# Per-head weight products in 16-bit passes: splitting raw weights on ScalarE and VectorE, with one raw buffer in place of two

## The reference

```
q_c = rmsnorm(hidden @ w_qa, g_qa)                # 384 latent columns
q   = q_c @ w_qb           -> q_nope (128), q_rope (64) for each of 32 heads
k_c = rmsnorm(kv[..., :128], g_kva)               # 128 latent columns
kst = k_c @ w_kvb          -> k_nope (128), v (128) for each head
scores = (query . key) * 192**-0.5                # nope and rope parts together
attn   = softmax(scores)
out    = (attn @ v) as 4096 columns @ w_o         # w_o: 4096 x 1024
```

## Time and profile before

| | |
|---|---|
| median of three timed runs | 2040.95 us |
| the profiled execution, its own time | 2044.69 us |
| its span | 2042.9 us |
| PE busy | 1892.5 us, 93% of the span |
| DVE busy | 1321.2 us, 65% |
| ACT busy | 773.2 us, 38% |
| POOL busy | 308.4 us, 15% |

### The profile page before, as it was taken

The page is one execution under the profiler, slowest core; times in us unless marked ns, Lnnn a source line. Parts: engine busy times, 40 slices in busy tenths (PEclk is TensorE's granted clock), DMA queues, the critical chain, the costliest instruction groups (busy, mean ns, idle before and its releaser), DMA issues. The chain is left out here.

```text
span 2042.9 us, 32412 instructions
## 1 busy us (share of the span) xinstructions
PE 1892.5 (93%) x11538; PEld 1029.6 (50%) x11538; DVE 1321.2 (65%) x2742; ACT 773.2 (38%) x2020; POOL 308.4 (15%) x596
## 2 busy tenths in 40 slices
PE   4898898559999999999999999999999999859999
PEld 2344444335555555555555555555555555425554
DVE  4678777436666666666666666666666666555554
ACT  3454554233333334433333433333343333332221
POOL 2376675300000000000000000000000000033332
PEclk9899999679999999999999999999999999979999
DMA  5244342332222322232222222223222222243332
GB/s 143 52 86 96 81 95 65 76 91 51 58 58 59 76 56 53 58 76 59 58 58 55 73 58 58 58 58 75 55 55 58 40 39 39 39 138 80 80 82 73
DMA packets 305609, 138.87 MB, mean 68 GB/s; under 512 B 295088, under 2 KB 295344, under 8 KB 303408
## 3 DMA queue, kind: packets, MB, share of 16 engines
q1 hardware_dynamic: 301136, 108.35, 24.8%
q10 hardware_dynamic: 4320, 28.51, 4.0%
HBM read 56.07 MB, written 8.39 MB: 32 GB/s over the span
## 5 line engine op out<-in xcount | busy, mean ns | idle before, releaser
L1031 PE MATMUL out_ps<-m_h,ot_h 128*128 128x512 f16 x1024 | 389.4, 380 | 1.7 <-DVE ot_l L835 1.7
L1032 PE MATMUL out_ps<-m_l,ot_h 128*128 128x512 f16 x1024 | 389.0, 380 | 0.0
L1033 PE MATMUL out_ps<-m_h,ot_l 128*128 128x512 f16 x1024 | 388.9, 380 | 0.0
L756 ACT ACTIVATE qp_h<-qp_ps 128x512 f16<-128x512 f32 x126 | 75.3, 597 | 492.6 <-PE qp_ps L966 492.6
L812 ACT ACTIVATE prob<-s_ps,nmx 128x128 f32<-128x128 f32 x512 | 181.3, 366 | 207.3 <-DVE nmx L905 207.3
L885 DVE SCALAR_TENSOR_TENSOR resid<-out_ps,resid 128x512 f32<-128x512 f32 x256 | 176.1, 688 | 97.1 <-PE out_ps L1033 97.1
L835 DVE SCALAR_TENSOR_TENSOR qp_l<-qp_ps,qp_h 128x512 f16<-128x512 f32 x126 | 87.2, 692 | 234.5 <-ACT qp_h L756 234.5
L1221 POOL MEMSET fpower<- 128x1 f32 x1 | 0.1, 99 | 1392.4 <-POOLq L674 1392.4
L966 PE MATMUL qp_ps<-lat,wp_h 128*128 128x512 f16 x756 | 205.6, 381 | 0.0
L1033 PEld LDWEIGHTS out_ps<-m_h,ot_l 128*128 128x128 f16 x1024 | 100.4, 98 | 121.6 <-issue 1.4
L1031 PEld LDWEIGHTS out_ps<-m_h,ot_h 128*128 128x128 f16 x1024 | 100.5, 98 | 110.5 <-DVE ot_l L835 2.7
(11 more groups left out here) (217 smaller groups left out, 3861.3 us busy)
## 6 DMA issues: line engine op xcount, KB each, us to landing
wide<-heads_in ACTq DMA_DIRECT2D x30, 928.0 KB, 4.7
wide<-x_in SPq DMA_DIRECT2D x30, 512.0 KB, 6.5
tower_out<-result SPq DMA_DIRECT2D x16, 512.0 KB, 2.6
stage<-wb_in SPq DMA_DIRECT2D x8, 512.0 KB, 8.3
resid<-wqk_in SPq DMA_DIRECT2D x1, 2304.0 KB, 11.6
zt<-z SPq DMA_TRANSPOSE x128, 2.4
turned<-halves SPq DMA_TRANSPOSE x128, 3.0
wide<-heads_in SPq DMA_DIRECT2D x2, 928.0 KB, 4.6
```

The lines of the kernel that those rows point to most:

```text
L756: act.activation(out, src, ACT.Copy, scale=scale).then_inc(done, 1)
L1031: pe.matmul(out_ps[hf][:, :], ot_h[:, h, :], m_h[:, at], start=h == 0, stop=False)
L1032: pe.matmul(out_ps[hf][:, :], ot_h[:, h, :], m_l[:, at], start=False, stop=False)
L1033: last = pe.matmul(out_ps[hf][:, :], ot_l[:, h, :], m_h[:, at], start=False, stop=h == HEADS - 1)
```

## The change

The raw weights of the heads whose products are made inside the rounds are split into 16-bit halves, and the product is made from them in three passes. For that the second raw buffer, wide1, is given up once the first four heads are done: its memory holds both halves of the 1664 columns w_q to w_o. The split is made in three pieces: 640 columns (w_q, w_k, w_v) in slot 0, and 512 each (the halves of w_o) in slots 1 and 2, so each piece is made one slot ahead of the part that reads it. On ScalarE a piece stands behind the split of the probabilities and ahead of the query's, on VectorE behind the additions of outputs and ahead of the query's split. The scale of the split, RAW_S = 2**8 on both operands, is taken out where the product is read. The load of the next head, now always into wide0, moves from the start of slot 0 to the start of slot 3, where the raw row has been split. The diff, cut to its core:

```
+        raw_hi, raw_lo = sem("raw_hi"), sem("raw_lo")
+        split = keep["wide1"][:, :].bitcast(F16)
+        split_h, split_l = split[:, 0:RAW_R], split[:, RAW_R:2 * RAW_R]
+        PIECES = [slice(RAW_Q, RAW_O), slice(RAW_O, RAW_O + CHUNK), slice(RAW_O + CHUNK, RAW_R)]
...
+            def raw_high(h, n):
+                if n == 0:
+                    act.wait_ge(raw_loaded[0], (h - HEADS) * 16 + 48)
+                    act.wait_ge(prod_done, h * 3)
+                    if h == HEADS:
+                        act.wait_ge(wr_lo, HEADS)
+                high(split_h[:, PIECES[n]], keep["wide0"][:, PIECES[n]], RAW_S, raw_hi)
...
             def body(before, now, after, more):
-                if more and (not now.known or now.t + HEADS + 1 < NH):
-                    act.wait_ge(prod_done, now.t * 3 + 3 * HEADS)
-                    act.wait_ge(wr_lo, now.t + HEADS)
-                    load(now.t + HEADS + 1, 1 - now.parity)
                 for j in range(QUAD):
                     s = now.slot + j
+                    if j == QUAD - 1 and now.t + HEADS + 1 < NH:
+                        act.wait_ge(wr_lo, now.t + HEADS + 1)
+                        act.wait_ge(raw_lo, now.t * 3 + 3)
+                        load(now.t + HEADS + 1, 0)
...
                     high(p_h, prob[:, :, :].rearrange("p h n -> p (h n)"), PR_S, p_hi)
+                    if more and j < len(PIECES):
+                        raw_high(now.t + HEADS, j)
                     if after:
                         query_high(after, j)
...
                         add_out(*behind, 1)
+                    if more and j < len(PIECES):
+                        dve.wait_ge(raw_hi, now.t * 3 + (j + 1))
+                        low(split_l[:, PIECES[j]], keep["wide0"][:, PIECES[j]], RAW_S, split_h[:, PIECES[j]], raw_lo)
                     if after:
                         query_low(after, j)
...
+            def split_products(h, part, bank, free):
+                pe.wait_ge(raw_lo, (h - HEADS) * 3 + (part + 1))
+                pe.wait_ge(prod_lo, free)
+                ways = ((split_h, split_h), (split_h, split_l), (split_l, split_h))
+                if part == 0:
+                    for k in range(QT):
+                        for n, (a, b) in enumerate(ways):
+                            last = pe.matmul(bank[:, k * P:(k + 1) * P], a[:, RAW_Q + k * P:RAW_Q + (k + 1) * P],
+                                             b[:, RAW_K:RAW_K + P], start=n == 0, stop=n == 2)
+                else:
+                    at = RAW_O + (part - 1) * CHUNK
+                    for n, (a, b) in enumerate(ways):
+                        last = pe.matmul(bank[:, :], a[:, RAW_V:RAW_V + P], b[:, at:at + CHUNK],
+                                         start=n == 0, stop=n == 2)
+                last.then_inc(prod_done, 1)
...
                     if more and j:
-                        products(now.t + HEADS, now.parity, j - 1, prod_ps, (now.t + HEADS) * 3 + (j - 1))
+                        split_products(now.t + HEADS, j - 1, prod_ps, (now.t + HEADS) * 3 + (j - 1))
```

More of the change, by code:

```diff
@@ L53 @@
 KR_S, QRO_S = 2.0**7, 2.0**7
+RAW_S = 2.0**8
 WP_S, WR_S, M_S = 2.0**9, 2.0**8, 2.0**10
@@ L758, in prod_high @@
             def prod_high(h, p, sd, k, part, bank, fresh):
+                un = 1.0 if fresh else RAW_S ** -2
                 act.wait_ge(prod_done, h * 3 + part + 1)
@@ L762, in prod_high @@
                     high(wp_h[:, bass.ds(sd, 1), :, bass.ds(k, 1), :].rearrange("p a t k n -> p (a t) (k n)"),
-                         bank[:, 0:QR].rearrange("p (t n) -> p t n", t=QT), WP_S, prod_hi)
+                         bank[:, 0:QR].rearrange("p (t n) -> p t n", t=QT), WP_S * un, prod_hi)
                     if not fresh:
@@ L771, in prod_high @@
                     high(m_h[:, bass.ds((sd * HEADS + k) * D + (part - 1) * CHUNK, CHUNK)], bank[:, :],
-                         M_S, prod_hi)
+                         M_S * un, prod_hi)
             def query_high(r, j, bank=qp_ps):
@@ L823, in body @@
                     if more and j:
-                        prod_high(now.t + HEADS, now.parity, now.side * -1 + 1, now.place, j - 1, prod_ps, False)
+                        prod_high(now.t + HEADS, 0, now.side * -1 + 1, now.place, j - 1, prod_ps, False)
                     act.wait_ge(av_done, s + 1)
@@ L836, in low, with prod_low @@
                                          op1=ALU.subtract).then_inc(done, 1)
-            def prod_low(h, p, sd, k, part, bank):
+            def prod_low(h, p, sd, k, part, bank, un=1.0):
                 dve.wait_ge(prod_hi, h * 3 + part + 1)
@@ L842, in prod_low @@
                     low(wp_l[at].rearrange("p a t k n -> p (a t) (k n)"),
-                        bank[:, 0:QR].rearrange("p (t n) -> p t n", t=QT), WP_S,
+                        bank[:, 0:QR].rearrange("p (t n) -> p t n", t=QT), WP_S * un,
                         wp_h[at].rearrange("p a t k n -> p (a t) (k n)"), prod_lo)
@@ L851, in prod_low @@
                     at = bass.ds((sd * HEADS + k) * D + (part - 1) * CHUNK, CHUNK)
-                    low(m_l[:, at], bank[:, :], M_S, m_h[:, at], prod_lo)
+                    low(m_l[:, at], bank[:, :], M_S * un, m_h[:, at], prod_lo)
             def query_low(r, j, bank=qp_ps):
@@ L926, in body @@
                     if more and j:
-                        prod_low(now.t + HEADS, now.parity, now.side * -1 + 1, now.place, j - 1, prod_ps)
+                        prod_low(now.t + HEADS, 0, now.side * -1 + 1, now.place, j - 1, prod_ps, RAW_S ** -2)
                     dve.wait_ge(o_hi, s + 1)
```

## The result

| | before | changed | ratio, 95% interval |
|---|---|---|---|
| first comparison, median (lowest to highest) | 2041.53 us (2040.42 to 2043.39) | 2026.24 us (2024.92 to 2026.98) | 0.9923 [0.9906, 0.9941] |
| repeated on another occasion | 2041.89 us (2038.42 to 2045.53) | 2027.00 us (2025.26 to 2029.45) | 0.9929 [0.9918, 0.9941] |

The changed kernel is faster by about 15 us, 0.7 to 0.8%. The forecast, 2029.9 us in a range of 2024.5 to 2035.5, had the direction and the range right and the gain too small by some 4 us.

A forecast was written before the change was run, and what follows sets the result against it. Two clocks bound the round: TensorE's sequence and a chain of splits beside it. Savings of 0.168 + 0.208 + 0.02 = 0.396 us a round, over 28 rounds 11.1 us, gave 2040.95 - 11.1 = 2029.9 us, range 2024.5 to 2035.5.

The forecast's parts named there:

- Product shorter by 0.168, 0.208 and 0.208 us: TensorE's product in slots 1, 2 and 3: 16-bit passes replace 32-bit records, 0.584 us less per head.
- The rival of weight loads that show: Slot 1: nine short passes take 0.88 us, losing 0.21 us and cancelling slot 2's gain; about 2040 us; 6%.
- The saving of slot 3 becomes a wait: End of slot 3: next scores wait 0.28 us for VectorE's query split, so the 0.208 us saved gains zero.
- The rival in which all of TensorE's saving arrives in the rounds: All slots with products: the query split's wait hides less, so 16.4 us are gained, 2024.6 us; 6%.
- The chain leaves slots 1 and 2 room: Softmax chain has 0.23 us to spare in slot 1, 0.21 in slot 2, so TensorE's savings there arrive whole.
- slot 1's saving seen one interval later: Sign in the transposes' issues: slot 1's saving appears in the following interval, about 10.55, 10.33, 10.70 us.
- The rival in which the chain takes the slots over: Slots 1 and 2: a 0.3 us longer softmax chain loses some 0.08 us each; 2034 us; 13% for such partial gains.
- Splits and raw load in the rounds at zero: New ScalarE and VectorE splits fit idle time with 3.1 and 1.0 us to spare; load lands 11 us early.
- the slower rival: Slot 0: ScalarE's raw piece waits for the single-buffer load; 2080 us with a load of 21 us; 3%.
- It is issued at the same point of a slot as before [...]. Zero.: Raw load moved to slot 3: meets the transpose of probabilities no more than before, so costs zero.

The follow-up runs named there:

- experiments 2 and 3: Changed kernel with a fourth product pass, low half by low half: in slot 3, 2029.31 us; in slot 2 instead, 2032.91 us.
- experiment 4: Changed kernel with queries ahead of outputs on TensorE and their splits ahead of raw pieces and additions: 2019.49 us.
- Experiment 7: Changed kernel with VectorE's split of each raw piece made three times: 2029.04 us.
- experiment 6: Changed kernel with VectorE's split of each raw piece made twice: 2026.44 us.
- experiment 5: Kernel before, 32-bit products kept, with only round 0's load of raw weights moved from the start of slot 0 to slot 3: 2038.09 us against 2040.41.
- experiment 1: Changed kernel run once more without any edit: 2027.00 us, against 2041.89 us for the kernel before.
- experiment 2: Changed kernel with a fourth product pass, low half by low half, in slot 3: 2029.31 us.
- the test of experiment 4: Version with queries ahead of the outputs, plus a fourth product pass in slot 3, against the kernel before: 2027.78 us, ratio 0.9938.

## Why the prediction was right, and where it fell short

- **Product shorter by 0.168, 0.208 and 0.208 us.** Right: 0.51, 0.64 and 0.65 us for the three parts, by the pace of the score and query passes of before. The rival of weight loads that show is out. The Trainium skill ("TensorE: Matmul & The Clock Gate", section "Back-to-back issue gap") gives a pace of about 81 ns for each pair of load and pass at 128 columns. This trace doesn't agree: nine of them took 0.51 us, 57 ns each.
- **The saving of slot 3 becomes a wait.** Right: experiments 2 and 3 show one pass to cost 0.02 us a round in slot 3 and 0.22 us in slot 2, experiment 4 with its test that the wait for the query's split is the reason. The rival in which all of TensorE's saving arrives in the rounds (16.4 us) is out, though the time came close to its 2024.6 us.
- **The chain leaves slots 1 and 2 room.** Right: the intervals were forecast as 10.12, 10.55, 10.33, 10.70 and came as 10.11, 10.54 to 10.55, 10.34, 10.70, with slot 1's saving seen one interval later. Experiment 7 found the spare time of slot 1 by using it up. The rival in which the chain takes the slots over is out: the round lost 0.415 us, no less than forecast.
- **Splits and raw load in the rounds at zero.** Right, with a whole second split to spare on VectorE (experiment 6). ScalarE waits for no load (no idle time ahead of its raw pieces in the groups above), so the slower rival is out.
- **"It is issued at the same point of a slot as before [...]. Zero."** This step failed. It was worked out in a round with others around it and for the transposes of probabilities, not for round 0 and its first rotary transpose: there the load was issued 0.93 us ahead of that transpose, and TensorE had nothing else to do while it waited. Moving the load took 1.8 us off (experiment 5). The row was in the trace of before: TensorE's single longest wait in the rounds, 5.56 us.
- **What stays open.** Rounds and first transpose make 11.6 + 1.8 = 13.4 us; the medians differ by 15.3 and 14.9. Both intervals reach down to 12 us (0.9941), so the remaining 1.5 to 2 us may be nothing, and no run shows a cause for them in the change. 15 runs of the kernel before on one chip spread over 4.9 us (2037.57 to 2042.51). The profiles show where single executions differ: in the time up to the first transpose, and in round 0 and round 31 by how long TensorE's granted clock stays at its lower level.

## What to carry to other kernels

When the engine that is busy all the time gets less work, work out slot by slot what is late next: the same 0.21 us was worth 0.21 us in one slot and 0.03 us in the next, because the next consumer hung on a split that was timed from the queries. Such a wait can then be removed by order alone: making the query earlier gave 7.5 us more, 5.3 of it in 28 rounds. And look at the first and the last round by themselves when something moves: a transfer that is hidden in every steady round may stand in front of the one that nothing hides.

## What the runs showed of the hardware

A bulk load held back a DMA transpose that was issued 0.93 us after it, on another queue: 4.25 us from issue to use in place of 2.45 (experiment 5) and 2.47 (the changed kernel).

TensorE's granted clock fell by the end of the wait for that first transpose, and did so in the shorter wait as well. TensorE's busy time and clock (columns as in the first view of this text) in the kernel before, which waited 5.56 us, until 449.10:

```profile
446.00:450.00 4.00, 0.90 (x9) 0.90 (x10) 0.00 (x0) 0.00 (x0) 0.00 (x0) 0.66 0.63 226
450.00:454.00 4.00, 4.00 (x17) 2.06 (x15) 2.70 (x8) 1.92 (x9) 0.00 (x0) 0.50 0.00 0
```

The passes behind the wait ran at 0.50, the level of 1.2 GHz. The changed kernel waited 3.77 us, until 443.98, with no load beside the transpose, and its clock was 0.50 from 444 to 446 too. How long it stays there differs between executions of one program. The changed kernel behind the next wait of round 0, for the first turned probabilities (reader at 453.71), and the same kernel once more in experiment 1 (reader at 454.19):

```profile
454.00:458.00 4.00, 4.00 (x31) 3.33 (x30) 1.55 (x3) 0.82 (x2) 0.00 (x0) 0.57 0.00 0
458.00:462.00 4.00, 4.00 (x22) 1.86 (x20) 3.26 (x9) 2.84 (x11) 0.00 (x0) 1.00 0.01 2
```

```profile
454.00:458.00 4.00, 3.81 (x25) 2.85 (x26) 0.87 (x2) 0.60 (x1) 0.00 (x0) 0.50 0.12 23
458.00:462.00 4.00, 4.00 (x19) 2.16 (x18) 2.87 (x9) 2.06 (x10) 0.00 (x0) 0.76 0.00 0
```

The first is back at full clock by 458, the second isn't: that goes with an interval of 11.34 us in the one and 12.28 in the other. In round 31 the same happens to some profiles and not to others: the intervals of 11.21 us (before), 11.40 (experiment 2), 11.30 (the split made three times) and 11.64 (the test of experiment 4) all hold a stretch at 0.50, behind waits of some 2 us, where the other profiles take 10.1 to 10.2 us.
